# Attention with a second score matmul, keys on partitions, in place of transposed probabilities

## The reference, cut to what matters

```
x  = x + tanh(g_xattn) * attention(layernorm(x), ctx)      # 16 batches, 224 queries, 750 keys, 512 wide
x  = x + tanh(g_ffn)   * experts(layernorm(x))             # untouched by the change

attention: Q = xn @ Wq + bq; K = ctx @ Wk + bk; V = ctx @ Wv + bv     # 16 heads of 32
           scores = Q K^T / sqrt(32) * gate[key]
           out    = softmax(scores) V @ Wo + bo
```

## Time and profile before

| | |
|---|---|
| median of 3 runs | 2177.83 us (2177.2 to 2179.82) |
| span of the profiled execution | 2176.1 us |
| attention, from the start to its last store's issue | about 1581 us |
| experts | about 595 us |
| PE busy over the span | 2043.5 us, 94% |
| DVE, ACT, POOL busy over the span | 58%, 44%, 27% |
| mean granted PE clock | 0.976 |

### The profile page before, as it was taken

One profiled execution on the slowest core, in us unless ns is written; L12 is line 12 of the kernel. 1 busy time (PEld: TensorE's weight loads), 2 busy tenths in 40 slices (PEclk: granted clock), 3 DMA queues, 4 the chain that ended last, 5 costly groups with the idle time before them and its releaser, 6 DMA issues. The chain is left out here.

```text
span 2176.1 us, 43249 instructions
## 1 busy us (share of the span) xinstructions
PE 2043.5 (94%) x13700; PEld 1677.6 (77%) x13701; DVE 1272.2 (58%) x2344; ACT 953.6 (44%) x1983; POOL 582.8 (27%) x682
## 2 busy tenths in 40 slices
PE   4999999999999999999999999999716999999999
PEld 4788888988888898888879888887514666678887
DVE  4557565665756566575666657565584333345555
ACT  0456565645656464565646556465411222210000
POOL 4222231322213132221313212130034333323331
PEclk9999999999999999999999999999956999999999
DMA  5645555554555555455555545554273444435543
GB/s 176 174 115 158 134 136 153 130 144 116 157 135 136 151 131 145 121 150 138 136 154 129 144 126 143 140 137 110 54 302 95 145 144 145 145 107 168 168 139 115
DMA packets 176438, 307.17 MB, mean 141 GB/s; under 512 B 29344, under 2 KB 86688, under 8 KB 176048
## 3 DMA queue, kind: packets, MB, share of 16 engines
q1 hardware_dynamic: 163008, 265.30, 44.4%
q0 software_dynamic: 10880, 33.56, 5.6%
q10 hardware_dynamic: 2512, 7.82, 0.9%
HBM read 145.03 MB, written 63.24 MB: 96 GB/s over the span
## 5 line engine op out<-in xcount | busy, mean ns | idle before, releaser
L631 DVE TENSOR_REDUCE neg_max<-score 112x1 f32<-112x750 f32 x512 | 455.9, 932 | 46.5 <-PE score L843 42.4
L463 ACT ACTIVATE probs<-score,neg_max 112x750 f32<-112x750 f32 x512 | 448.1, 883 | 74.1 <-DVE neg_max L631 72.7
L866 PE MATMUL flip<-ident,probs 112*125 112x112 f32 x3072 | 420.6, 274 | 9.3 <-ACT probs_t L471 8.2
L471 ACT ACTIVATE probs_t<-flip 125x448 f32<-125x448 f32 x512 | 276.6, 543 | 328.4 <-PE flip L866 328.0
L866 PEld LDWEIGHTS flip<-ident,probs 112*125 112x125 f32 x3072 | 387.4, 188 | 41.6 <-ACT probs_t L471 15.7
L361 POOL TENSOR_TENSOR k_lo<-fresh,k_hi 128x376 fp32r<-128x376 f32 (+1 forms) x128 | 118.2, 923 | 448.3 <-ACT k_hi L491 448.3
L843 PE MATMUL score<-k_stack,q_stack 128*112 128x512 f32 (+1 forms) x1024 | 232.7, 348 | 3.2 <-ACT probs L463 3.2
L815 PE MATMUL proj<-ctx_hi,wk_hi 128*128 128x376 f32 (+1 forms) x512 | 183.7, 359 | 8.3 <-POOL ctx_lo L361 6.2
L639 DVE TENSOR_SCALAR probs_t<-flip 125x448 f32<-125x448 f32 x256 | 158.1, 617 | 45.8 <-PE flip L866 45.6
L815 PE MATMUL proj<-ctx_lo,wk_hi 128*128 128x376 f32 (+1 forms) x512 | 172.0, 336 | 0.0
L815 PE MATMUL proj<-ctx_hi,wk_lo 128*128 128x376 f32 (+1 forms) x512 | 171.9, 336 | 0.0
(11 more groups left out here) (189 smaller groups left out, 3175.9 us busy)
## 6 DMA issues: line engine op xcount, KB each, us to landing
k_stack<-k_hi SPq DMA_DIRECT2D x512, 93.8 KB, 2.2
k_stack<-k_lo SPq DMA_DIRECT2D x512, 93.8 KB, 2.2
q_stack<-q_parts SPq DMA_DIRECT2D x128, 224.0 KB, 3.6
ctx_raw<-in_ctx_t SPq DMA_DIRECT2D x64, 375.0 KB, 5.3
y_slots<-y_sb SPq DMA_DIRECT2D x72, 256.0 KB, 3.1
x_in<-in_x SPq DMA_DIRECT2D x16, 448.0 KB, 5.5
q_parts<-q_hi SPq DMA_DIRECT2D x64, 112.0 KB
q_parts<-q_lo SPq DMA_DIRECT2D x64, 112.0 KB
```

The costliest lines, as they stand in the source:

```text
L463: act.activation(probs[0:QW, h % 2, t, :], score[t][0:QW, 0:S], ACT.Exp, bias=neg_max[:, h % 2, t:t + 1], accum_out=row_sum[:, t, h:h + 1] ...
L471: act.activation(probs_t[0:KW, h % HC, 2 * p:2 * p + 2, :].rearrange("k a q -> k (a q)"), flip[(3 * h + p) % 2][0:KW, 0:2 * L], ACT.Relu). ...
L631: nc.vector.tensor_reduce(neg_max[:, h % 2, t:t + 1], score[t][0:QW, 0:S], axis=AX.X, op=ALU.max, negate=True).then_inc(maxed[t], 1)
L866: ins = nc.tensor.transpose(flip[g % 2][0:KW, k * L + t * QW:k * L + (t + 1) * QW], probs[0:QW, h % 2, t, kt * KW:(kt + 1) * KW], ident[0: ...
```

## The change

The probabilities are no longer transposed. The scores are computed twice. The first time (`score_rows`) is as before but with 96 contraction rows (K hi, K hi, K lo against Q hi, Q lo, Q hi) and into one PSUM tile for both query halves, and serves only for the maximum. The second time (`score_columns`) has the keys as weights, 125 at a time, and all 224 queries as moving operand, so that keys come out on partitions. Two more contraction rows subtract the maximum: `k_stack` holds ones there, and `q_stack` the negated maximum's rounded part and remainder. The unit of this is a "tick": for one head two key tiles, that is two matmuls into one of two banks `st`, and one exponential of 125x448 straight into `probs_t`. A chunk has 12 ticks, in three phases of four heads; after each phase `attend` runs a third of the product with V.

The row sums now come from POOL, which adds the `probs_t` tiles of a head into `acc` (20 additions of 125x224 for a chunk, `add_first`, `add_left`, `add_right`), and from `sum_up`, four pairs of matmul records with a column block of ones. DVE takes the reciprocal of 128x224 from PSUM. To bring the maximum into the contraction, DVE splits it (`split_shift`), PE turns it (`turn_shift`), DVE copies it (`copy_shift`) and a DMA on ACT's queue places it (`place_shift`).

```diff
-        score = [ps(f"score{t}", [P, 1024]) for t in range(QT)]
-        flip = [ps(f"flip{i}", [P, 512]) for i in range(2)]
-        proj = ps("proj", [P, 512])
-        pv = ps("pv", [P, 512])
+        score = ps("score", [P, 1024])
+        st = [ps(f"st{i}", [P, 512]) for i in range(2)]
+        proj = [ps(f"proj{i}", [P, 512]) for i in range(2)]
+        pv = [ps(f"pv{i}", [P, 512]) for i in range(2)]
...
+            def exponential(b, c, u):
...
+                        act.wait_ge(pv_done, phases(b, c, p) - 1)
+                    act.wait_ge(added, ticks(b, c, u) - 2 * HC + 1)
+                act.activation(probs_t[0:KW, (c * PHASES + p) % 2, u % HC, :], st[u % 2][0:KW, 0:2 * L], ACT.Exp)\
+                    .then_inc(exped, 1)
...
+            def place_shift(b, c):
+                act.wait_ge(shift_read, b * DC + c + 1)
...
+                act.dma_start(q_stack[ROWS:SHIFTED, c * HC:(c + 1) * HC, :].bitcast(F32).rearrange("r j q -> r (j q)"),
+                              shift_rows[:, :]).then_inc(shift_in, 16)
...
+            def score_columns(b, c, u):
...
+                if u == 0:
+                    pe.wait_ge(shift_in, 16 * (b * DC + c + 1))
+                if not (fixed and ticks(b, c, u) < 2):
+                    pe.wait_ge(exped, ticks(b, c, u) - 1)
+                h = c * HC + u % HC
...
+                    kt = u // HC * 2 + k
+                    ins = nc.tensor.matmul(st[u % 2][0:KW, k * L:(k + 1) * L], k_stack[0:SHIFTED, h, kt * KW:(kt + 1) * KW],
+                                           q_stack[0:SHIFTED, h, :], start=True, stop=True)
+                ins.then_inc(st_done, 1)
...
+                score_columns(b, 2, 0)
+                next_scores(b, 14, 0)
+                if not last:
+                    project_k(n, "K1a", b, (2, 4))
+                score_columns(b, 2, 1)
+                if not last:
+                    project_k(n, "K1b", b, (0, 1))
+                next_scores(b, 14, 1)
+                attend(b, 1, 2)
```

More of the change, by code:

```diff
@@ new lines, in batch @@
+                for u in range(TICKS):
+                    exponential(b, 1, u)
+                    if u == 3:
+                        keep_positive(b, 0, b, not first)
+                    if not last and u == 4:
+                        split_high(n, "K0a", b)
+                    if not last and u == 7:
+                        split_high(n, "Q0", b)
+                    if u == 9:
+                        place_shift(b, 2)
+                        if not last:
+                            split_high(n, "K0b", b)
@@ new lines, in project_q @@
+            def project_q(i, b, steps):
+                bank = take_proj(b, f"Q{i}") if steps[0] == 0 else proj[bank_of(b, f"Q{i}")]
+                for step in range(*steps):
+                    k, d = divmod(step, DC)
+                    c = 2 * i + k
+                    ins = nc.tensor.matmul(bank[:, k * L:(k + 1) * L], wq_sb[:, d, c * P:(c + 1) * P], xn_t[:, d, :],
+                                           start=(d == 0), stop=(d == DC - 1))
+                if steps[1] == 2 * DC:
+                    ins.then_inc(proj_done, 1)
@@ new lines, in project_v @@
+            def project_v(kt, b, chunks):
+                name = f"V{kt}"
+                bank = take_proj(b, name) if chunks[0] == 0 else proj[bank_of(b, name)]
+                for d in range(*chunks):
+                    for k, (xp, wp) in enumerate(((ctx_hi, wv_hi), (ctx_hi, wv_lo), (ctx_lo, wv_hi))):
+                        ins = nc.tensor.matmul(bank[0:KW, :], xp[:, d, kt * KW:(kt + 1) * KW], wp[:, d, :],
+                                               start=(d == 0 and k == 0), stop=(d == DC - 1 and k == 2))
+                if chunks[1] == DC:
+                    ins.then_inc(proj_done, 1)
@@ new lines, in project_out @@
+            def project_out(m, t, b, chunks):
+                name = f"O{t}"
+                bank = take_proj(b, name) if chunks[0] == 0 else proj[bank_of(b, name)]
+                for c in range(*chunks):
+                    if t == 0:
+                        pe.wait_ge(normed, m * DC + c + 1)
+                    ins = nc.tensor.matmul(bank[0:QW, :], out_t[:, c, t * QW:(t + 1) * QW], wo_sb[:, c, :],
+                                           start=(c == 0), stop=(c == DC - 1))
+                if chunks[1] == DC:
+                    ins.then_inc(proj_done, 1)
@@ L962, in _ @@
             batch(B - 1, False, True)
+            attend(B - 1, 3, 2)
+            sum_up(B - 1, 3)
             for t in range(QT):
[L964 to L965 removed]
+                project_out(B - 1, t, B, (0, 4))
+            for t in range(QT):
+                turn_result(B - 1, t, B)
+            for t in range(QT):
+                route(t, B)
 TOP, MID = 2, 128
```

1404 lines of the change are left out of this document (888 added, 516 removed).

## The result

The changed kernel takes 2553.55 us against 2177.51 us, a ratio of 1.1726 with a 95% interval of 1.1712 to 1.174. It is 17% slower; the forecast was 2075 us, faster. The profiled execution has a span of 2547.3 us.

What follows compares the result with a forecast made beforehand. PE bounds attention; the experts stay unchanged. Attention's end: 92 setup + 78 first batch + 14 batches of 88 (1232) + 52 last + 5 = 1459 us against 1562, hence 2075 us; 8-in-10 range 2035 to 2148.

Steps and rivals of the forecast that it cites:

- The pitch: Time of one batch in the attention loop, forecast to go from 94.6 us to 88 us.
- w: PE's new waits per batch in the attention loop, added to its 86.9 us of work; taken as 1.1 us.
- For w I take 1.1 us, between 0 and 6.: Step pricing PE's new waits per batch on other engines and transfers: 1.1 us, bounds 0 and 6.
- three signs of being wrong: Column matmuls stepping at 0.15 us or more, `score_rows` waiting over 6 us a batch, or first tick after 105 us.
- No row shows POOL slowed by them.: Remark on DVE instructions with two SBUF inputs contending with POOL: few exist, no profile row shows slowing; no time added.
- The key copies ... come in time by the same row.: Key copies into `k_stack` fall from 64 to 48 and arrive in time, by a 2.2 us copy row.
- of K1a and K3a I expect DVE to come free just as PE wants the next tile: Third chunk: POOL's queued remainders delay DVE's `read_split` and maxima, with DVE free just in time; no separate price.
- I take 0.11 us each, 10.6 us.: PE's 96 added column matmuls per batch: 0.11 us each, 10.6 us together, bounds 9.5 and 18.0 us.
- the profile gives 15.7 us of them: PE's waits for copied transpose pieces, said to vanish: 15.7 us over 16 batches, 1.0 us a batch.
- Outside the pitch: Attention outside the regular batches: first tick at 92 us, batch 0 78 us, last batch 52 us, then 5 us.
- DVE's or POOL's order stalls PE: Rival: one 1.5 us wait per chunk makes w 6 or 7, giving 2158 us; 14 in 100.
- The shift's transfer: The DMA on ACT's queue placing the negated maximum: 2 to 4 us, hidden before PE wants it.

Runs made afterwards that it cites:

- e11: e9 with DVE doing `add_result(b, 1)` ahead of `next_maximum(b, 10, 0)`; 2407.51 us, ratio 1.1049.
- e1: The changed kernel with the reciprocal kept in PSUM, so `normalize_output`'s last product has one SBUF input; 2588.52 us, ratio 1.1893.
- e2: The changed kernel with POOL's additions cut to 8 of 224 columns, most of the row sums left out; 2456.58 us, ratio 1.1287.
- e3: The changed kernel with SP issuing a chunk's twelve key copies before its query copies and the wait for stored queries; 2515.26 us, ratio 1.1556.
- e5: The changed kernel with the edits of e1 and e3, and the Newton steps moved from DVE to POOL; 2461.08 us, ratio 1.1306.
- e9: e5 with a separate semaphore for key copies, so ACT's rounding of K2a and K3a doesn't wait for query copies; 2398.33 us, ratio 1.1011.
- e10: e9 with each pair of column matmuls issued twice into the same tile; 2482.35 us, ratio 1.1404.
- e8: e5 with `project_out` and Q pieces joined into two blocks each, and POOL's additions cut to 8 columns; 2476.79 us, ratio 1.1378.

## Why the prediction was wrong

The pitch, 116.1 us against 88, comes apart into three terms. The waits above 0.5 us with a releaser in that batch are 4.74, 2.11, 1.63, 0.55, 0.51, 6.56 and 1.56, together 17.7 us, where w was 1.1: +16.6. The columns took 16.6 us where 10.6 was forecast: +6.0. The rest of PE's instructions, 116.1 - 17.7 - 16.6 = 81.8 us, were forecast at 86.9 - 10.6 = 76.3: +5.5. In e11 the columns take 15.5 us and the same rest 105.8 - 11.9 - 15.5 = 78.4, at a granted clock of 0.95 against 0.90. So the rest was priced within some 2 us, and the clock makes up most of the third term and a part of the second.

- **The step that failed: "For w I take 1.1 us, between 0 and 6."** It is out of its bounds by a factor of three, and it draws the clock after it. Two parts of it were argued wrongly, and e1, e2, e3, e5 and e9 show them: DVE was taken to be free beside POOL, where it was held for 4.15 us before a maximum that PE waits for (4.74 us), and SP's queue was taken to cost nothing, where PE waits 6.56 us behind it. Of the prediction's own three signs of being wrong only the first tick's came, 113.7 us; the columns step at 0.11, and `score_rows` waits 54.6 us in all, 3.4 a batch.
- **"No row shows POOL slowed by them."** True of the kernel before, and the lesser half of the question. I asked whether DVE would slow POOL, in a kernel whose POOL was busy 27%. With POOL at some 60% it is DVE that stands where it matters, and DVE's maxima are what PE waits for; POOL is slowed too, 1.35 us for an addition behind the context remainder. The Trainium skill's rule of contention for instructions of two SBUF inputs, cited with the rivals, was the right one to price. The Trainium skill says more in "SBUF — State Buffer", section "SBUF: two separate sides": the pair of ports is an exclusive lock, taken for a whole instruction, and the loser blocks fully. The trace agrees for the context remainder and the shift's, which stood for one instruction of POOL. For the product and the Newton step, 4.15 and 5.21 us, it differs: one whole instruction of POOL would have been 0.66 or 1.76 us, and these two did not get in between POOL's instructions until POOL paused.
- **"The key copies ... come in time by the same row."** The landing time is right, 2.2 us in both pages. What was left out is the queue: a chunk's twelve copies cost SP 0.62 us each to issue, behind query copies and stores. The two slots of `k_hi` turn that into a chain over ACT, POOL and DVE to PE. I named this chain ("of K1a and K3a I expect DVE to come free just as PE wants the next tile") and gave it no price.
- **"I take 0.11 us each, 10.6 us."** Right for the matmul (e10), short for the places where it stands. I had seen 0.07 us on entering a float32r group in the earlier trace rows, and used it for `attend` alone. Of the batch's 48 pairs 29 have float32 work before or behind them or fall in a stretch of low clock, and take 0.29 to 0.82 us where 0.22 is two steps.
- **DVE and POOL.** The reciprocal was forecast at 1.5 us and takes 1548 ns; POOL's addition at 0.54 us and takes 663 to 687 ns, so POOL stands at 68 us a batch and not 59. That made its unbroken stretches longer; by e2 and e8 their length matters through the hold, and without it no more than the intervals show.
- **"the profile gives 15.7 us of them".** This row is the idle time of the weight loads. PE's own waits for the copied pieces are 8.2 us over the kernel before, 0.5 us a batch and not 1.0; the sum should have been 87.4 us, and the third term is then 5.0.
- **Outside the pitch.** The first tick came at 113.7 us, not 92: PE waited 22.1 us there for maxima in a single score tile. From it to the last `project_out` (1937.8 us) lie 1824.1 us against 1367: 14 pitches of 116.6 give 401 of the 457, batch 0 and the last one the other 56. The last does end as forecast: `sum_up` waits 7.3 us for POOL's additions.
- **The rivals.** The right mechanism, "DVE's or POOL's order stalls PE", had 14 in 100, and its price of 1.5 us a chunk was a third of the true one. The shift's transfer cost PE 0.2 us in all; that part was hidden, as forecast.

What no run settles: how much of the loss a better order could give back. e9 recovered 155 of 376 us. In e11's batch PE's own work is 93.9 us with every wait taken out, against 94.6 for the whole pitch before. So by this estimate a perfect order of this version would gain about 1 us a batch at that clock, and some 3 if the rest took the forecast's 76.3 beside e11's 15.5 for the columns; neither was run, nor what the work would take at the full clock of the kernel before. No version run here comes near the kernel before.

## What to carry to other kernels

When a change moves work to an engine that was idle, ask what that engine's unbroken stretches do to its neighbours, not only whether its total fits. Look for every instruction on the other side that could be held, since taking one away can hand the hold to the next, as in e1. Count the issuing queue of every small transfer, and ask which buffer's reuse waits for the last of them. Where four engines stand in turn behind one transfer, its lateness reaches PE in full. Price a matmul with the neighbours that it will have, and look at the granted clock behind PE's idle stretches, since they can cost more than their length.

## What the runs showed of the hardware

- Some DVE instructions with two SBUF inputs were held while POOL ran SBUF to SBUF instructions back to back: 0.39 us of work took up to 4.3 us, and a two-element product 5.21 us, through three to seven instructions of POOL, whose additions kept their 0.66 us. Others of the kind got in after the one under way: the shift's remainder (0.62 us) and the context remainder (0.96 us, and 1.35 for POOL's addition behind it). With one of the inputs in PSUM the same product took 392 ns each time.
- After 4.7 us of idle PE the granted clock of the next 6 us was 0.72, after 6.6 us it was 0.50 over 8 us; one `project_out` matmul took 592 ns at the upper and 1196 at the lower level. Taking 34.6 us from the largest wait came with 63 us less (e9), taking 39.2 from it with 38 (e3), and adding 10.6 us of matmuls a batch cost 5.6 (e10).
- A pair of float32r matmuls of 224 columns takes 0.22 us to the next start among its kind, 0.31 beside `attend`, 0.38 beside Q's float32 matmuls of 224 columns and 0.62 beside `project_out`'s of 512.
